# A decoder layer on one core: the transposed row maxima of self attention take a turn in the three banks of the score maxima

## The reference, cut to what matters

```python
q, k, v = (_heads(q), _heads(k), _heads(x))
scores = jnp.einsum('bhqd,bhkd->bhqk', q, k) * scale
scores = jnp.where(causal, scores, -jnp.inf)
y_ar = jnp.einsum('bhqk,bhkd->bhqd', jax.nn.softmax(scores, axis=-1), v)
...
ma = jnp.einsum('bhqd,bhkd->bhqk', qa, ka)
```

## Time and profile before

| what | before |
|---|---|
| median of three runs | 1773.21 us |
| span of the profiled execution | 1773.4 us |
| TensorE busy in it | 1681.7 us, 95% |
| VectorE busy | 1254.6 us, 71% |
| ScalarE busy | 974.2 us, 55% |
| GpSimd busy | 1161.8 us, 66% |

### The profile page before, as it was taken

How to read it: one execution, slowest core, us unless ns; L and a number is a source line. 1 busy time by engine, 2 the same in 40 slices (tenths; PEclk the granted TensorE clock), 3 DMA queues, 4 the chain that set the end, 5 groups by cost and what they waited for, 6 DMA issues and landing times.

```text
span 1773.4 us, 30895 instructions
## 1 busy us (share of the span) xinstructions
PE 1681.7 (95%) x10626; PEld 1111.0 (63%) x10626; DVE 1254.6 (71%) x2785; ACT 974.2 (55%) x1939; POOL 1161.8 (66%) x964
## 2 busy tenths in 40 slices
PE   5999999999999989999998999999999999999998
PEld 4766666666666547877863556566565656656566
DVE  5677777777777666767876776877778686777745
ACT  4555555555555443433445565656666665666554
POOL 2556556556555554744565977878788786878874
PEclk9999999999999989999998999999999999999999
DMA  6556555555555464576625543535344354534210
GB/s 199 147 149 168 145 152 156 153 156 165 141 153 153 122 194 152 181 219 185 193 66 155 144 115 88 139 90 155 91 114 114 82 138 99 144 93 108 63 42 31
DMA packets 167273, 237.29 MB, mean 134 GB/s; under 512 B 22087, under 2 KB 73287, under 8 KB 167117
## 3 DMA queue, kind: packets, MB, share of 16 engines
q1 hardware_dynamic: 167116, 235.31, 48.2%
HBM read 91.57 MB, written 41.94 MB: 75 GB/s over the span
## 4 chain that ended last, share of the span: by engine, by line
PE 68%; DVE 12%; POOL 8%; DMA 4%; issue 4%; ACT 2%; SPq 1%; POOLq 0%; DVEq 0%; ACTq 0%
PE bank L1652 9%; POOL cross_added L1974 7%; PE bank L201 5%; PE bank L202 5%; PE bank L203 5%; DVE bank L585 5%; PE bank L1522 5%; PE bank L1490 5%; PE bank L1461 5%; PE bank L369 4%; PE bank L305 4%; PE bank L356 3%; DVE bank L548 2%; PE bank L1558 2%; PE bank L329 2%
## 5 line engine op out<-in xcount | busy, mean ns | idle before, releaser
L1471 DVE TENSOR_REDUCE cross_negmax<-bank 128x1 f32<-128x512 f32 x512 | 338.7, 674 | 149.8 <-PE bank L1461 147.2
L1738 ACT ACTIVATE cpt<-bank 128x512 f32<-128x512 f32 x512 | 297.7, 595 | 143.6 <-PE bank L1490 140.1
L548 DVE CUSTOM_DVE_ANT_0 bank<-bank,future 128x128 f32<-128x128 f32 (+3 forms) x512 | 243.0, 488 | 177.8 <-PE bank L356 177.7
L430 ACT ACTIVATE pt<-bank 128x256 f32<-128x256 f32 (+3 forms) x512 | 217.5, 444 | 260.2 <-PE bank L305 256.1
L1974 POOL TENSOR_TENSOR cross_added<-cross_added,cpt 128x2048 f32<-128x2048 f32 x61 | 280.0, 4591 | 11.5 <-ACT cpt L1738 11.0
L618 POOL TENSOR_SCALAR_AFFINE_SELECT pt<-pt 128x512 f32<-128x512 f32 x128 | 81.1, 634 | 246.8 <-ACT pt L430 246.8
L1490 PE MATMUL bank<-cqk 98*128 98x512 f32 x512 | 227.4, 444 | 7.1 <-ACT cpt L1738 6.2
L1461 PE MATMUL bank<-cqk 96*128 96x512 f32 x512 | 212.5, 418 | 10.7 <-DVE cross_negmax L1471 8.6
L1974 POOL TENSOR_TENSOR cross_added<-cpt,cpt 128x2048 f32<-128x2048 f32 x32 | 146.6, 4581 | 84.0 <-ACT cpt L1738 84.0
L305 PE MATMUL bank<-qk 98*128 98x256 f32 (+2 forms) x512 | 180.6, 359 | 8.4 <-ACT pt L430 3.9
L356 PE MATMUL bank<-qk 96*128 96x256 f32 (+2 forms) x512 | 169.5, 335 | 4.4 <-DMA qk<-stage 4.4
(11 more groups left out here) (207 smaller groups left out, 3623.8 us busy)
## 6 DMA issues: line engine op xcount, KB each, us to landing
qk<-stage SPq DMA_DIRECT2D x384, 128.0 KB, 2.3
cqk<-cstage SPq DMA_DIRECT2D x384, 128.0 KB, 2.3
scratch_memory<-memory SPq DMA_DIRECT2D x32, 512.0 KB, 3.8
ma<-scratch_memory SPq DMA_DIRECT2D x32, 512.0 KB, 3.9
raw<-in_x_t SPq DMA_DIRECT2D x32, 256.0 KB, 2.9
v<-in_x SPq DMA_DIRECT2D x32, 256.0 KB, 3.2
scratch_y_ar<-y_ar SPq DMA_DIRECT2D x32, 256.0 KB, 2.4
my_ar<-scratch_y_ar SPq DMA_DIRECT2D x32, 256.0 KB, 4.6
```

Of the source, the lines that this page charges most:

```text
L548: dve.tensor_tensor_reduce(out=scores, in0=scores, in1=sh.future[:, SEQ - P * (qt + 1):SEQ], scale=-1.0, scalar=-NEG, op0=ALU.add, op1=ALU ...
L1471: dve.reduce_max(s.negmax[gm % 2][:, col:col + 1], max_bank(sh, m)[:, :], AX, negate=True).then_inc(s.dve_max, 1)
L1738: act.activation(s.pt[step % 3][:, j, :], sh.bank[2 + n % 2][:, :], ACT.Exp, scale=SCALE_CROSS).then_inc(s.act_exp, 1)
```

## The change

A transpose of the maxima no longer goes to bank 6 or 7 but takes a turn in the ring of banks 0, 1 and 5, as a seventeenth entry after every sixteen scores. `max_place(m)` is the place of score m in that sequence and `shift_place(d)` that of the transpose of group d; the bank is the place modulo three. Each entry waits until the entry three places before has been read: `max_bank_free` waits for its maximum, or for `dve_sh` where that entry is a transpose. The transpose itself waits for the maximum of the score two before the latest one (`dve_max` at 16(d+1)+1), which is the one three places before.

K's first matmul and the sums no longer wait for `dve_sh`; K's waits for the norm of the group before. `LATE_NORM` is gone: in groups 29 and 30 the norm comes in slots (1,0) to (2,0), as everywhere.

```diff
-LATE_NORM = NG - 3
-def shift_bank(sh, d):
-    return sh.bank[7 if d > LATE_NORM else 6]
+AHEAD = SELF_LEAD + 11 - 2 * SLOTS
+def max_place(m):
+    return m + max(0, (m - AHEAD) // SLOTS)
+def shift_place(d):
+    return SLOTS * (d + 1) + AHEAD + d
+def max_bank_self(sh, place):
+    return sh.bank[SELF_MAX[place % 3]]
+def max_bank_free(pe, s, place):
+    before = place - 3
+    if before < 0:
+        return
+    turn, at = divmod(before - AHEAD, SLOTS + 1)
+    if at == SLOTS and turn >= 0:
+        pe.wait_ge(s.dve_sh, turn + 1)
+    else:
+        m = before - max(0, turn)
+        pe.wait_ge(s.dve_max, m + 1)
...
             if d + 4 > NG:
-                pe.wait_ge(s.dve_sh, min(d + 2, NG))
                 pe.wait_ge(s.dve_norm, NORM * d)
...
-            pe.wait_ge(s.dve_max, n16 * (d + 1))
-            if g == LATE_NORM:
-                pe.wait_ge(s.act_k2, 2 * NG - 1)
-            elif g > LATE_NORM:
-                pe.wait_ge(s.dve_sh, g + 1)
-            elif g >= 1:
-                pe.wait_ge(s.dve_norm, NORM * g)
-            else:
-                pe.wait_ge(s.dve_k, g + 3)
-            pe.transpose(shift_bank(sh, d)[0:n16, 0:P], s.negmax[d % 2][:, :], sh.ident[:, :]).then_inc(s.pe_sh, 1)
+            pe.wait_ge(s.dve_max, min(n16 * (d + 1) + 1, NS))
+            pe.transpose(max_bank_self(sh, shift_place(d))[0:n16, 0:P], s.negmax[d % 2][:, :],
+                         sh.ident[:, :]).then_inc(s.pe_sh, 1)
...
-    kq, bank = s.kq[g % 3], sh.bank[SELF_MAX[m % 3]]
+    kq, bank = s.kq[g % 3], max_bank_self(sh, max_place(m))
...
-    if m >= 3:
-        pe.wait_ge(s.dve_max, m - 2)
+    max_bank_free(pe, s, max_place(m))
...
-        elif g >= 2:
-            pe.wait_ge(s.dve_sh, g - 1)
-        elif g == 1:
-            pe.wait_ge(s.dve_k, 1)
+        elif g >= 4:
+            pe.wait_ge(s.dve_norm, NORM * (g - 3))
+        elif g >= 1:
+            pe.wait_ge(s.dve_k, g)
...
-        if 0 <= g - 1 < NG and not LATE_NORM <= g < NG - 1:
+        if 0 <= g - 1 < NG:
             self_norm(dve, s, sh, g - 1, PER * kt + j - PER)
...
-        if LATE_NORM <= g < NG - 1:
-            self_norm(dve, s, sh, g - 1, PER * kt + j - 11)
```

More of the change, by code:

```diff
@@ L463, in self_scalar @@
                 act.wait_ge(s.shift_landed[(d - 1) % 3], 32 * ((d - 1) // 3 + 1))
-            act.activation(s.shift[:, 0, :].bitcast(F32R), shift_bank(sh, d)[0:PER * TILES, 0:P],
+            act.activation(s.shift[:, 0, :].bitcast(F32R), max_bank_self(sh, shift_place(d))[0:PER * TILES, 0:P],
                            ACT.Copy).then_inc(s.act_sh, 1)
@@ L546, in self_vector @@
             col = jm * TILES + qt
-            scores = sh.bank[SELF_MAX[m % 3]][:, 0:P * (qt + 1)]
+            scores = max_bank_self(sh, max_place(m))[:, 0:P * (qt + 1)]
             dve.tensor_tensor_reduce(out=scores, in0=scores, in1=sh.future[:, SEQ - P * (qt + 1):SEQ], scale=-1.0,
@@ L562, in self_vector @@
             dve.wait_ge(s.act_sh, d + 1)
-            dve.tensor_tensor(hl[:, 1, :].bitcast(F32R), shift_bank(sh, d)[0:PER * TILES, 0:P], hl[:, 0, :],
+            dve.tensor_tensor(hl[:, 1, :].bitcast(F32R), max_bank_self(sh, shift_place(d))[0:PER * TILES, 0:P], hl[:, 0, :],
                               ALU.subtract).then_inc(s.dve_sh, 1)
-        if LATE_NORM <= g < NG - 1:
-            self_norm(dve, s, sh, g - 1, PER * kt + j - 11)
         if kt == 3 and j == 2 and 0 <= g + 3 < NG:
```

## The result

The changed kernel took 1777.81 us (median of six runs) against 1772.93 us for the kernel before in as many: a ratio of 1.0030, with a 95% interval from 1.0018 to 1.0042. Measured once more on another chip (12 runs against 17) it was 1.0016, from 1.0004 to 1.0028. The change makes the kernel slower by 0.2 to 0.3%. The forecast was +6.9 us and 1780.1 us; measured were +4.9 and +3.1 us.

A forecast was written before the change was run, and what follows sets the result against it. TensorE bounds the kernel, each group's length set by VectorE's chain up to TensorE's last release plus TensorE's own work. Terms 5.3 + 1.6 = 6.9 us gave 1780.1 us for the median, +0.39%, range 1774.7 to 1785.7.

The forecast's parts named there:

- The moved stall: Slot (2,3), groups 1 to 28: TensorE's wait moves from transpose to score, 0.19 us later per group, 5.3 us in all.
- The rule on rotating banks: Ring of three banks: matmul groups should rotate through different banks; spoke against lending the transpose a turn, gave no price.
- Nothing else moved in the middle groups: Middle groups: waits for `dve_sh` have 1.6 us of cover, stores maybe 0.2 us later; removing K's wait gains nothing.
- The last groups: Groups 29 to 31: norm moved earlier delays stores by 0.6 us and group 30 by 1.0, together +1.6 us.
- rival C: Last groups dearer: TensorE idles in (2,2) and (2,3) of group 29, clock falls; 1784.3 us, chance 0.15.
- The term of group 30: Group 30: transpose 1.2 us later, GpSimd's wait absorbs 0.23 us; +1.0 us, bounds 0 and 1.5.
- the step on the clock: Behind group 29: TensorE's clock may fall or recover earlier; effect taken as zero, 2.5 us left on either side.
- The basis: Whole kernel: the profiled span of 1773.4 us was taken as 0.2 us above the median of the runs.
- A: Middle groups: maximum of (2,1) ready when TensorE asks, so 14.5 us won, last groups lose 1.6; 1760.3 us, chance 0.07.
- B: Moved stall costs 2.5 us since weight loading is hidden, and last groups absorb theirs; 1775.7 us, chance 0.23.

The follow-up runs named there:

- the kernel with the product later: Changed kernel with the norm's product moved from slot (2,0) to (2,3), behind the shift's remainder; ratio 0.9951 to the kernel before, 1761.2 us against 1771.1.

## Why the prediction was right or wrong

**The moved stall: right, in place and size.** The wait went from the transpose to the score of (2,3), and the score came later than before, since its maximum stands behind the product on VectorE. The step gave 0.19 us per group with bounds of 0.09 and 0.25; measured were 0.184. In the rows of one group 0.10 is the later start (1.15 against 1.05 us after the product's start), and 0.11 the longer way to L382 (0.43 against 0.32). The two make 0.21, of which 0.03 come back in the rest of the group. The step had put them at 0.09 and 0.10. In the other direction, taking the product out of the chain gave 0.37 us and spreading the reciprocals 0.28 more, so it is the chain that sets a group's length.

**The rule on rotating banks**, from the Trainium skill, "Perfetto Trace Analysis", section Matmuls, spoke against the change and was right on its direction. But the banks alone don't make the loss: with the same three banks the kernel with the product later is 0.5% faster than before. It is the combination with VectorE's order.

**Nothing else moved in the middle groups: right.** Neither `dve_sh` ahead of the score of (3,1) nor the landing of the stores (2.3 us, as before) shows up as a wait of TensorE there.

**The last groups: wrong, +1.6 us forecast, -0.9 us in the traces.** In group 29 the step held up to the stores. VectorE's chain from (1,0) to the end of L576 is 7.96 us instead of the forecast 7.7, and the stores go out 615.53 - 607.50 = 8.03 us after its start against 7.09, 0.94 us later where the step had 0.6 with a bound of 1.0. What failed is "all of it reaches TensorE, since it waits for their landing". TensorE doesn't wait for it any more. It idles in (2,2) and (2,3) instead (0.90, 0.58 and 0.35 us), the clock goes to 0.50 there, the 16 matmuls of L382 take 3.22 us where they took 1.71 before, and TensorE itself arrives after the landing: no wait stands on its row at 619.81.

From the chain's start to the next (0,0) it is 619.81 - 607.50 = 12.31 us, against 613.89 - 603.24 = 10.65, so 1.66 us are lost, about rival C's mechanism. But the slow stretch is then over when group 30 begins. From there to its sums it takes 622.79 - 619.81 = 2.98 us at full clock, against 618.63 - 613.89 = 4.74 us at half: 1.76 us given back. The stretch of low clock is about as long in both and merely lies over other work. The prediction had left 2.5 us on either side for this and taken zero. The sums of group 30 in the trace before:

```profile
618.63 1.77 PE L329 MATMUL bank<-self_added,ones 128*32 128x512 f32 x8
```

The term of group 30, forecast at +1.0, failed as well, though the chain behaved as forecast. The transpose comes 628.65 - 624.37 = 4.28 us after the chain's start against 624.04 - 620.93 = 3.11, the forecast 1.2 us later, and TensorE waits 1.18 us for it. Yet from the sums of group 30 to those of group 31 it is 637.45 - 622.79 = 14.66 us, against 633.31 - 618.63 = 14.68. About 0.7 us come back at the very start: the sums of group 30 took 1.70 us to the next matmul before, at a granted clock of 0.50 (618 to 620 us), and 0.98 us after, at 1.00 (622 to 624 us). Where the other 0.5 us come back was not followed. Behind that the prediction had no term, and nearly all of the 0.9 us was gained there: from the sums of group 31 to the last ones it is 16.09 us against 16.88, at a mean granted clock of 0.81 against 0.68. Which part of these 0.8 us is clock and which is order wasn't separated. The prediction's own sign had named the case: if the stretch behind group 29 is shorter, the step on the clock is wrong.

**The basis.** The prediction set the median at the span less 0.2 us. That was wrong: a run is about 1.9 us longer than its span (1775.45 and 1773.6 us for the profiled one of the changed kernel). The span before, 1773.4 us, thus belongs to one of the slower executions. It cost nothing here, since the sum was a difference.

**The rivals.** A, the wait simply goes, fell for the reason given: TensorE asks before VectorE has finished the product. That the maximum of (2,1) decides is shown by the kernel with the product later, which is A's condition almost met. B's premise for the middle groups, weights that cost nothing, is refuted by the 0.11 us, and 0.184 us per group is twice its price. On the last groups B was right, they absorb theirs. Its total, 2.5 us, is below the first measurement of 4.9, but the second, 3.1 with an interval from 0.7 to 5.0 us, doesn't exclude it; the traces do. C's mechanism in group 29 came true, but what it cost there came back in group 30.

## What to carry to other kernels

Before a wait is removed, find the item of the other engine's chain that releases this engine next. If it lies behind the item waited for now, the stall only changes its name, and a bank lent from a ring can make that next item a later one. Then look at what the removed wait had forced into that order: here the gain of 1.1% came from moving work that no longer had to be early out of the chain, not from the removal itself. Read the waits of the weight loads beside those of the matmuls, since a short wait can hide behind the tail of the matmul before.

## What the hardware showed that was not expected

A score matmul that had to wait for VectorE cost TensorE 0.10 to 0.11 us beyond the wait, in the kernel before and after. The low clock in the last groups lasted about as long in both kernels, but whether it fell on the weights of group 29 or on the first slots of group 30 moved about 1.7 us back and forth between neighbouring groups. And the shift's stores of 8 KB took from 1.8 to 3.0 us (medians) to land, the longer the closer they were issued behind a store of 512 KB; that this store is the cause was not tested.
